# LayerNorm, attention and a routed low-rank layer on 8 cores: elementwise steps moved from GpSimd to VectorE, and the exponential and the product with V issued in halves

## The reference

```python
xn = (x - mean) / sqrt(var + 1e-5)                     # x: 4 x 2048 x 2048
q, k, v = (xn @ W.T for W in (Wq, Wk, Wv))             # 16 heads of 128
attn = softmax(q @ k.T * 128**-0.5) @ v                # no mask
base = xn @ W_base.T + b_base
e    = argmax(xn @ router_W.T)                         # 8 experts
h    = (xn @ A[e].T)                                   # rank 16
y    = x + attn @ Wo.T + base + 2.0 * (h @ Bw[e].T)
```

## Time and profile before

| | us |
|---|---|
| median of 2 runs | 1330.44 (1326.93 to 1333.95) |
| the profiled execution | 1331.08 |
| its span, slowest core (core 5) | 1329.5 |
| spans of the 8 cores | 1316.0 to 1329.5 |
| PE busy | 1133.9 (85%) |
| ACT busy | 487.8 (37%) |
| DVE busy | 419.6 (32%) |
| POOL busy | 136.3 (10%) |

### The profile page before, as it was taken

One profiled execution on the slowest core, in us unless ns is written; L12 is line 12 of the kernel. 1 busy time (PEld: TensorE's weight loads), 2 busy tenths in 40 slices (PEclk: granted clock), 3 DMA queues, 4 the chain that ended last, 5 costly groups with the idle time before them and its releaser, 6 DMA issues.

```text
span 1329.5 us, 14722 instructions; the slowest of 8 cores (1316.0 to 1329.5 us)
## 1 busy us (share of the span) xinstructions
PE 1133.9 (85%) x5266; PEld 472.5 (36%) x5266; DVE 419.6 (32%) x481; ACT 487.8 (37%) x419; POOL 136.3 (10%) x104
## 2 busy tenths in 40 slices
PE   4510899999999999989898989999999999989977
PEld 1100333333333343434343434333333343434433
DVE  2389642222221313130404040313131312234335
ACT  4501044435352626261616262534344444430000
POOL 1144120100101000000000101010101010001110
PEclk9855999999999999999999999999999999989989
DMA  8950094515152433433333333341515150309996
GB/s 236 283 52 0 1 134 42 48 16 48 18 47 24 41 34 32 38 37 36 34 32 32 32 33 34 30 45 19 48 17 48 17 48 2 31 1 138 178 165 183
DMA packets 174773, 77.56 MB, mean 58 GB/s; under 512 B 168432, under 2 KB 168432, under 8 KB 172656
## 3 DMA queue, kind: packets, MB, share of 16 engines
q0 software_dynamic: 168656, 51.42, 37.6%
q1 hardware_dynamic: 3744, 16.82, 4.7%
q10 hardware_dynamic: 2304, 8.39, 1.6%
HBM read 111.26 MB, written 8.39 MB: 90 GB/s over the span
## 4 chain that ended last, share of the span: by engine, by line
PE 69%; DMA 11%; ACT 9%; DVE 7%; issue 4%; ACTq 0%; POOL 0%; DVEq 0%; SPq 0%; POOLq 0%
PE PC L547 8%; PE PD L653 8%; PE PD L613 8%; PE PC L600 8%; PE PA L587 8%; PE PB L480 8%; PE PA L480 8%; DMA arena<-x 7%; PE PB L527 4%; ACT arena L534 4%; DMA y<-arena 4%; PE PA L527 3%; DVE xn_s L363 2%; DVE xn_s L379 1%; DVE arena L351 1%
## 5 line engine op out<-in xcount | busy, mean ns | idle before, releaser
L542 DVE TENSOR_TENSOR arena<-arena 128x1024 bf16<-128x1024 bf16 x240 | 166.2, 692 | 221.0 <-ACT arena L534 221.0
L547 PE MATMUL PC<-arena 128*128 128x512 bf16 x512 | 152.2, 378 | 55.4 <-ACT arena L534 32.0
L534 ACT ACTIVATE arena<-PB,consts 128x1024 bf16<-128x1024 f32 x128 | 154.4, 1206 | 54.9 <-PE PB L527 41.7
L534 ACT ACTIVATE arena<-PA,consts 128x1024 bf16<-128x1024 f32 x128 | 154.8, 1209 | 34.4 <-PE PA L527 34.4
L653 PE MATMUL PD<-xn_s,arena 128*128 128x512 bf16 x512 | 139.8, 380 | 0.0
L571 ACT CAST arena<-PA 128x1024 bf16<-128x1024 f32 x16 | 16.2, 1013 | 283.9 <-PE PB L480 221.2
L587 PE MATMUL PA<-xn_s,arena 128*128 128x512 bf16 x480 | 106.0, 379 | 12.5 <-ACT arena L571 12.5
L600 PE MATMUL PC<-xn_s,arena 128*128 128x512 bf16 x512 | 113.1, 379 | 0.0
L613 PE MATMUL PD<-xn_s,arena 128*128 128x512 bf16 x512 | 113.1, 379 | 0.0
L515 DVE CAST arena<-PB 128x1024 bf16<-128x1024 f32 x16 | 19.6, 1225 | 275.3 <-PE PB L511 275.3
L480 PE MATMUL PB<-xn_s,arena 128*128 128x512 bf16 x480 | 106.0, 379 | 0.0
(11 more groups left out here) (112 smaller groups left out, 952.0 us busy)
## 6 DMA issues: line engine op xcount, KB each, us to landing
arena<-x SPq DMA_DIRECT2D x8, 1024.0 KB, 8.3
arena<-x POOLq DMA_DIRECT2D x8, 1024.0 KB, 8.3
arena<-wk POOLq DMA_DIRECT2D x16, 512.0 KB, 11.2
arena<-wq POOLq DMA_DIRECT2D x16, 512.0 KB, 8.9
arena<-wv POOLq DMA_DIRECT2D x16, 512.0 KB, 8.0
arena<-x SPq DMA_DIRECT2D x16, 512.0 KB, 5.8
arena<-wb POOLq DMA_DIRECT2D x16, 512.0 KB, 7.9
arena<-wo POOLq DMA_DIRECT2D x16, 512.0 KB, 10.8
```

What stands on the lines that cost most here:

```text
L534: return s.activation(p_sb[:, (tkc % 2) * SO:(tkc % 2 + 1) * SO], src[:, 0:SO], AF.Exp, bias=ck("shift"), scale=ck("scale"))
L542: return v.tensor_add(dst, dst, pc_)
L547: last = t.matmul(PC[:, o0:o0 + w], lhsT=vt_sb[:, tkc * 128:(tkc + 1) * 128], rhs=p_sb[:, (tkc % 2) * SO + o0:(tkc % 2) * SO + o0 + w], st ...
```

## The change

The subtraction and the multiplication of all 16 chunks are on VectorE. `expev_f` is issued twice per step, for columns 0 to 511 and 512 to 1023, each half with a name of its own (`p0q0`, `p0q1`, `p1q0`, `p1q1`). `av_f` issues one matmul, and is emitted twice per step; each half reads its own half of the probabilities, and both write `@PC`. `collapse_f` still works on the whole and reads both halves' names.

```diff
-            eng = "gpsimd" if c % 4 == 3 else "vector"
-            p.emit(eng, sub_m, reads=["mb", f"xn{c}"], writes=[f"xn{c}"])
+            p.emit("vector", sub_m, reads=["mb", f"xn{c}"], writes=[f"xn{c}"])
...
-            meng = "gpsimd" if c % 4 == 2 else "vector"
-            p.emit(meng, mul_r, reads=["rb", f"xn{c}"], writes=[f"xn{c}"])
+            p.emit("vector", mul_r, reads=["rb", f"xn{c}"], writes=[f"xn{c}"])
...
-        def expev_f(s, tkc):
+        def expev_f(s, tkc, o0, w):
             src = PSBT[tkc % 2]
-            return s.activation(p_sb[:, (tkc % 2) * SO:(tkc % 2 + 1) * SO],
-                                src[:, 0:SO], AF.Exp, bias=ck("shift"), scale=ck("scale"))
+            return s.activation(p_sb[:, (tkc % 2) * SO + o0:(tkc % 2) * SO + o0 + w],
+                                src[:, o0:o0 + w], AF.Exp, bias=ck("shift"), scale=ck("scale"))
...
-        def av_f(t, tkc):
-            last = None
-            for (o0, w) in _slices(SO):
-                last = t.matmul(PC[:, o0:o0 + w],
+        def av_f(t, tkc, qi):
+            (o0, w) = _slices(SO)[qi]
+            return t.matmul(PC[:, o0:o0 + w],
...
-                p.emit("scalar", (lambda s, tkc=tkc, f=expev_f: f(s, tkc)),
-                       reads=[PSKEY[tkc % 2], "consts"], writes=[f"p{tkc % 2}"])
+                for (qi_, (qo0_, qw_)) in enumerate(_slices(SO)):
+                    p.emit("scalar", (lambda s, tkc=tkc, o0=qo0_, w=qw_, f=expev_f: f(s, tkc, o0, w)),
+                           reads=[PSKEY[tkc % 2], "consts"], writes=[f"p{tkc % 2}q{qi_}"])
...
-                    p.emit("tensor", (lambda t, tkc=tkc, f=av_f: f(t, tkc - 1)),
-                           reads=[f"p{(tkc - 1) % 2}", "vt"], writes=["@PC"])
+                    for qi_ in range(len(_slices(SO))):
+                        p.emit("tensor", (lambda t, tkc=tkc, qi=qi_, f=av_f: f(t, tkc - 1, qi)),
+                               reads=[f"p{(tkc - 1) % 2}q{qi_}", "vt"], writes=["@PC"])
```

More of the change, by code:

```diff
@@ L542, in collapse_f @@
             return v.tensor_add(dst, dst, pc_)
-        def av_f(t, tkc):
-            last = None
-            for (o0, w) in _slices(SO):
-                last = t.matmul(PC[:, o0:o0 + w],
[L548 to L551, removed]
+        def av_f(t, tkc, qi):
+            (o0, w) = _slices(SO)[qi]
+            return t.matmul(PC[:, o0:o0 + w],
+                            lhsT=vt_sb[:, tkc * 128:(tkc + 1) * 128],
+                            rhs=p_sb[:, (tkc % 2) * SO + o0:(tkc % 2) * SO + o0 + w],
+                            start=(tkc == 0), stop=(tkc == nT - 1))
         for h in range(H):
@@ L661, in build @@
                        reads=["ksb", "qsb", PSKEY[tkc % 2]], writes=[PSKEY[tkc % 2]])
-                p.emit("scalar", (lambda s, tkc=tkc, f=expev_f: f(s, tkc)),
-                       reads=[PSKEY[tkc % 2], "consts"], writes=[f"p{tkc % 2}"])
+                for (qi_, (qo0_, qw_)) in enumerate(_slices(SO)):
+                    p.emit("scalar", (lambda s, tkc=tkc, o0=qo0_, w=qw_, f=expev_f: f(s, tkc, o0, w)),
+                           reads=[PSKEY[tkc % 2], "consts"], writes=[f"p{tkc % 2}q{qi_}"])
                 p.emit("vector", (lambda v, tkc=tkc, h=h, f=collapse_f: f(v, tkc, h)),
-                       reads=[f"p{tkc % 2}", f"sumacc{h % 2}"], writes=[f"sumacc{h % 2}"])
+                       reads=[f"p{tkc % 2}q0", f"p{tkc % 2}q1", f"sumacc{h % 2}"], writes=[f"sumacc{h % 2}"])
                 if tkc >= 1:
-                    p.emit("tensor", (lambda t, tkc=tkc, f=av_f: f(t, tkc - 1)),
-                           reads=[f"p{(tkc - 1) % 2}", "vt"], writes=["@PC"])
+                    for qi_ in range(len(_slices(SO))):
+                        p.emit("tensor", (lambda t, tkc=tkc, qi=qi_, f=av_f: f(t, tkc - 1, qi)),
+                               reads=[f"p{(tkc - 1) % 2}q{qi_}", "vt"], writes=["@PC"])
                 if tkc == 1:
@@ L674, in build @@
                            reads=[kwb, "xn", "@PD"], writes=["@PD"])
-            p.emit("tensor", (lambda t, f=av_f: f(t, nT - 1)),
-                   reads=[f"p{(nT - 1) % 2}", "vt"], writes=["@PC"])
+            for qi_ in range(len(_slices(SO))):
+                p.emit("tensor", (lambda t, qi=qi_, f=av_f: f(t, nT - 1, qi)),
+                       reads=[f"p{(nT - 1) % 2}q{qi_}", "vt"], writes=["@PC"])
             def baev(v, h=h):
```

## The result

The changed kernel takes 1379.23 us (median of 11 runs, 1373.54 the fastest) where the kernel before takes 1332.45 (median of 10 runs made with them): 1.0352 times as long, 95% interval 1.0331 to 1.0374. It is slower, as half of the chances had it, and 22 us above the predicted 1357, 1.2 us outside the range. The profiled execution took 1380.15, its span is 1378.5 on core 2 and 1362.8 to 1378.5 over the cores. In some executions the cores of one die are granted a lower clock: the ratios leave these executions out, the medians have them in, and where a profile has such cores (0 to 3 in `no_self_wait` and in the last four kernels of the table) its stages are read from cores 4 to 7.

A forecast was written before the change was run, and what follows sets the result against it. TensorE, 69% of the chain of waits, was taken as the bound. Moving elementwise steps gave -22.2 us, the halves +48.5 over 16 heads: +26.3 on 1331.08, so 1357 us, range 1337 to 1378.

The forecast's parts named there:

- Edit 1: Between statistics and first head: moving eight subtractions and multiplications from GpSimd to VectorE gives 22.2 us, 20 to 24 kept.
- The stall of line 351: Before the heads: this one-partition product on VectorE takes 2.28 instead of 16.84 us, everything behind coming 14.56 earlier.
- the four and twelve subtractions: Before the heads: two batches on VectorE at 1.16 us each, the first 1.16 longer, the second 13.9 in all.
- The halves: Head loop: exponential and product probabilities x V each in two halves cost +3.03 us a head, +48.5 over 16 heads.
- Self-wait: Product in each step: its second half waits for its first on TensorE, 0.535 us start to start, 0.32 over 0.215.
- a step: Middle of a head: 1.825 us instead of 1.617, seven matmuls at 1.505 plus 0.32, no exponential waited for.
- the tail: End of a head, to the next head's first matmul: 6.48 us instead of 6.02, +0.46.
- the middle: Ten steps of a head from its second product: 18.25 us instead of 16.17, +2.08.
- the start: Head's start, to the second product: two pairs of exponential halves delay the copy of V by 0.245 each, +0.49 us.
- Rivals A and B: Product's second half: A, waiting for the first costs nothing, 1323 us; B, it costs 0.415, 1374 us; chance 0.12 each.
- Heads 1 to 15 do not show it now: Head starts: only head 0 loses TensorE's full clock in the kernel before; the sum kept the others at full clock.
- Rival C: Head starts: TensorE falls to its lower clock in a sparse stretch 0.5 us longer, 1.7 a head, 1383 us; chance 0.07.

The follow-up runs named there:

- `no_self_wait`: Changed kernel, with the two halves of the product writing names of their own so the second does not wait for the first: 1327.47 us, ratio 0.9982.
- the last four kernels of the table: Changed kernel again, 1374.88 us; kernel before again, 1337.36; kernel before with elementwise steps and V's second-half copy on VectorE, 1299.89; that with four residual buffers, 1299.04.
- experiment 3: Kernel before with only the product probabilities x V in two halves, both writing `@PC`, exponential whole: 1393.62 us, ratio 1.0489.
- experiment 2: Kernel before with only the exponential in two halves, both written before the whole product: 1365.38 us, ratio 1.0287.
- experiment 7: Changed kernel plus four redundant matmuls in each head while TensorE waits for the copy of V: 1358.08 us, ratio 1.0233.
- experiment 8: Changed kernel with four buffers instead of two for the residual in the last stage: 1367.81 us, ratio 1.0292.
- experiment 5: Kernel before with exponential and product both in halves, GpSimd keeping its eight elementwise steps: 1399.74 us, ratio 1.0532.
- edit 1 alone: Kernel before with only the subtractions and multiplications of all chunks on VectorE, head loop unchanged: 1303.98 us, ratio 0.9819.

## Why the prediction was wrong, point by point

**Edit 1, right.** Predicted -22.2; measured -23.1 in the start of the heads and -24.3 alone. The stall of line 351 and the four and twelve subtractions (4.61 and 13.71) came as worked out; the first router group is 23.7 us earlier on the slowest core where 22.3 was predicted.

**The halves, right in every term.** Self-wait 0.535 predicted, 0.52 measured; half of the exponential 0.78 and 0.777; a step 1.825 and 1.82; the tail 6.48 and 6.46; a head +3.03 and +3.01, 48.2 us over 16. In heads without a spell, the middle from the second product to that of step 11 is 18.20 (18.25 predicted), and the start from scores 0 to the second product grew from 4.15 to 4.63 (+0.49 predicted). The Trainium skill, "ScalarE: Activation LUTs", section "What ACT_TABLE_LOAD costs", has a formula for an activation, 186 ns and 93 for each operand given by pointer and 0.833 a column. That is an estimate of 0.80 us for the half with two such operands; the row has 0.777, so trace and page agree within 3%, and the fixed part is what halves pay twice.

**Rivals A and B, wrong.** The self-wait is neither free nor 0.415: start to start is 0.52, not 0.215 and not 0.63.

**The step that failed: "Heads 1 to 15 do not show it now".** The sum kept TensorE at its full clock in all heads but the first. Rival C, with a chance of 0.07, is what happened, in ten heads of sixteen and at 1.42 us instead of 1.7 for each: 14 us, where it had 26. Its own condition, a sparse stretch 0.5 us longer, is only half of it. The step behind the copy has also become thinner, and experiment 3 shows that this alone brings spells in half of the heads, while the longer start alone (experiment 2) brings them in 2.6; the forecast looked at the longer gap and not at the density of what follows. The direct evidence is experiment 7, where more work at the same pitch took all spells away. In chance terms the mistake was to give the rival little weight on the ground that heads 1 to 15 are at full speed now, while head 0 showed how near the edge they are.

**A term that was missing: the last stage.** The sum had only the last head's own share in it, 2.5 us behind its copy. Measured were 12.3. Of the other 9.8 about 1 is the spell of head 15, which six of the eight cores have and which ends behind its copy; for the rest stands the round over two buffers, whose wait grew by 9.6 (experiment 8). TensorE is also at its lower clock for 19.8 us of this stage instead of 10.6, and no run separates that from the waits.

By the means over the cores the parts add up: -23.1 for edit 1, +48.2 for 16 heads, +13 for the spells between the first and the last copy (58.4 measured there, less 15 times 3.01), +9.8 for the last stage, 47.9. The mean span grew by 48.0, from 1322.8 to 1370.8. By this mean the profiled execution is the longest of eleven (1363.7 to 1370.8), so the part that scatters most, the last stage, is probably at its upper end in it.

**Open.** Why one head falls and its neighbour with the same instructions doesn't. It isn't the DMA load, though that was 0.53 in head 6 and 0.16 in head 5: over heads 1 to 15 of all cores, heads with a spell have shares from 0.04 to 0.61 and heads without one from 0.07 to 0.63. The spells come in a pattern, in every second head on most cores with the product's halves alone, in two of three heads on most cores in experiment 5; so the moment at which a head starts may decide, which no run tests. And why the last stage's round is slower in the changed kernel than with edit 1 alone.

## What to carry to other kernels

Where waits are made from names, splitting one group into two that write the same name puts a wait of the engine on itself between them: give each part its own name, or expect up to 0.3 us a split where the engine is the bound, 49 us here with the spells that it brought. Halving an activation pays its fixed part twice, so it only helps where the consumer really stands waiting for the first half. When TensorE's work has a sparse stretch per iteration, ask whether a few idle-time matmuls keep its clock up, and take away what it waits for before splitting what it computes: the copy on the idle VectorE gained 1 us a head, the halves lost 3.

## What the runs showed of the hardware

- A wait of TensorE on its own last matmul costs 0.52 us from start to start with 512 columns, against 0.215 back to back. In stage 1, where a wait for ScalarE stands ahead of it, it was 0.63; in the changed kernel a wait for ScalarE stands ahead of it too, and it is 0.52.
- TensorE's clock fell to half in stretches where it never stood still for longer than 1.43 us (head 5 of the changed kernel), or, with the product's halves alone, than 0.92 us (experiment 3), and four redundant matmuls, 1.02 us in a gap, prevented it in all 16 heads of all cores. The Trainium skill, "TensorE: Matmul & The Clock Gate", section "Part 1: The HAM clock gate", calls the throttled state the default that activity releases; that the fall went away with more activity agrees.
- Elementwise operations on GpSimd with both inputs in SBUF held up one on VectorE: four in a row, 16.06 us, made it last 16.84 instead of 2.27 us. The Trainium skill, "GPSIMD Engine Reference", section "Specifications", says that the two engines share their way to SBUF; the trace agrees, in this form and size.
